# Moving the products of probabilities and values one slot later in an attention and feed-forward kernel

## The reference

```python
c = x @ W.T + b + lora(x, adapter of the sequence)       # cond
q, k, v = c @ wq, c @ wk, c @ wv                         # 32 query heads, 8 k/v heads of 128
q, k = rope(q), rope(k)
p = softmax(mask(q @ k.T * 128**-0.5))                   # causal, within each sequence of 64
x = x + (p @ v) @ wo                                     # attention
m = x @ W2.T + gated lora                                # cond2, top 2 of 8
x = x + m @ base_w.T + base_b + gated lora               # ffn, top 2 of 16
```

## Time and profile before

| what | value |
|---|---|
| median of 3 runs | 2785.87 us (2785.77 to 2792.49) |
| the profiled execution | 2785.09 us, of which 2783.0 us from first to last instruction (the span) |
| TensorE busy with matmuls | 2698.9 us, 97% of the span |
| VectorE, ScalarE, GpSimd busy | 1353.2, 857.3, 1187.6 us |
| mean granted TensorE clock | 0.990 of full speed |

### The profile page before, as it was taken

The page is one execution under the profiler, slowest core; times in us unless marked ns, Lnnn a source line. Parts: engine busy times, 40 slices in busy tenths (PEclk is TensorE's granted clock), DMA queues, the critical chain, the costliest instruction groups (busy, mean ns, idle before and its releaser), DMA issues.

```text
span 2783.0 us, 37584 instructions
## 1 busy us (share of the span) xinstructions
PE 2698.9 (97%) x14520; PEld 2179.5 (78%) x14520; DVE 1353.2 (49%) x2019; ACT 857.3 (31%) x2089; POOL 1187.6 (43%) x782
## 2 busy tenths in 40 slices
PE   8989999999999999999999999999999999999999
PEld 7877777777777788887877777777777778888877
DVE  3134677667777111124533577777777711112552
ACT  2132344444444211221212334444444421121110
POOL 0035765555655245510304475565555434451020
PEclk9999999999999999999999999999999999999999
DMA  6953122122215333111544312222212443311322
GB/s 220 225 184 113 54 76 77 57 69 72 69 62 188 129 114 109 51 39 55 142 123 122 98 54 74 71 77 76 73 57 69 174 136 106 114 46 38 90 87 68
DMA packets 312498, 268.48 MB, mean 96 GB/s; under 512 B 68730, under 2 KB 283898, under 8 KB 312322
## 3 DMA queue, kind: packets, MB, share of 16 engines
q1 hardware_dynamic: 250722, 210.50, 25.1%
q10 hardware_dynamic: 61600, 55.58, 6.0%
HBM read 201.88 MB, written 64.16 MB: 96 GB/s over the span
## 4 chain that ended last, share of the span: by engine, by line
PE 86%; POOL 6%; ACT 3%; DMA 2%; issue 1%; SPq 1%; DVE 1%; ACTq 0%; POOLq 0%; DVEq 0%
PE prod L673 26%; PE prod L675 25%; PE prod L674 25%; PE turned L919 3%; PE turned L869 2%; POOL s_lo L1496 2%; ACT probs L1254 1%; POOL o_lo L1531 1%; PE turned L667 1%; ACT s_hi L1222 1%; PE turned L902 1%; PE prod L1105 1%; POOL w_lo L1461 1%; POOL w_sum L1521 1%; DMA raw<-in_wo 1%
## 5 line engine op out<-in xcount | busy, mean ns | idle before, releaser
L1461 POOL TENSOR_TENSOR w_lo<-raw,w_hi 128x1024 fp32r<-128x1024 f32 x96 | 239.1, 2492 | 815.2 <-ACT w_hi L1165 815.2
L673 PE MATMUL prod<-o_hi,w_hi 128*128 128x512 f32 x1024 | 402.5, 393 | 12.2 <-POOL o_lo L1531 8.6
L675 PE MATMUL prod<-o_hi,w_lo 128*128 128x512 f32 x1024 | 398.7, 389 | 0.0
L674 PE MATMUL prod<-o_lo,w_hi 128*128 128x512 f32 x1024 | 398.6, 389 | 0.0
L1496 POOL TENSOR_TENSOR s_lo<-w_sum,s_hi 128x512 fp32r<-128x512 f32 x192 | 254.4, 1325 | 259.8 <-ACT s_hi L1222 259.8
L1820 DVE TENSOR_TENSOR x<-prod,x 128x512 f32<-128x512 f32 x128 | 88.5, 692 | 562.3 <-PE prod L675 562.3
L673 PE MATMUL prod<-t_hi,s_hi 128*128 128x512 f32 x768 | 314.2, 409 | 12.2 <-POOL s_lo L1496 12.2
L1165 ACT CAST w_hi<-raw 128x1024 fp32r<-128x1024 f32 x130 | 136.0, 1049 | 609.8 <-PE prod L675 431.5
L675 PE MATMUL prod<-t_hi,s_lo 128*128 128x512 f32 x768 | 301.8, 393 | 0.0
L674 PE MATMUL prod<-t_lo,s_hi 128*128 128x512 f32 x768 | 301.3, 392 | 0.0
L673 PE MATMUL prod<-b_hi,s_hi 128*128 128x512 f32 x576 | 241.4, 419 | 0.0
(11 more groups left out here) (168 smaller groups left out, 5067.2 us busy)
## 6 DMA issues: line engine op xcount, KB each, us to landing
raw_pair<-in_wq SPq DMA_DIRECT2D x64, 512.0 KB, 3.6
o_scratch<-o_out ACTq DMA_DIRECT2D x64, 512.0 KB, 2.9
raw<-in_wo SPq DMA_DIRECT2D x64, 512.0 KB, 3.9
o_raw<-o_scratch SPq DMA_DIRECT2D x64, 512.0 KB, 7.1
raw<-t_scratch SPq DMA_DIRECT2D x50, 512.0 KB, 3.6
t_scratch<-x ACTq DMA_DIRECT2D x17, 512.0 KB, 5.6
x_raw<-in_x SPq DMA_DIRECT2D x16, 512.0 KB, 5.8
xt_scratch<-x_sum SPq DMA_DIRECT2D x16, 512.0 KB, 3.3
```

The costliest lines, as they stand in the source:

```text
L673: pe.matmul(dst, wh, xh, start=start, stop=False)
L674: pe.matmul(dst, wh, xl, start=False, stop=False)
L675: return pe.matmul(dst, wl, xh, start=False, stop=stop)
L1461: pool.tensor_tensor(WL[i % 2][:], RAW[i % 2][:], WH[i % 2][:].bitcast(F32), ALU.subtract).then_inc(w_lo, 1)
```

## The change

Five of the items in the two lists, TensorE's and ScalarE's, stand one slot later. No instruction is added, removed or altered.

```diff
                                 if at_ == (QD_KV, 5):
                                     turn_p(gg - 1, 1, 0)
-                                if at_ == (QD_KV, 6):
+                                if at_ == (QD_01, 0):
                                     pv(gg - 1, 0, 0)
-                                if at_ == (QD_01, 0):
+                                if at_ == (QD_01, 1):
                                     turn_p(gg - 1, 1, 1)
-                                if at_ == (QD_01, 1):
+                                if at_ == (QD_01, 2):
                                     pv(gg - 1, 0, 1)
-                                if at_ == (QD_01, 3):
+                                if at_ == (QD_01, 4):
                                     pv(gg - 1, 1, 0)
-                                if at_ == (QD_01, 5):
+                                if at_ == (QD_01, 6):
                                     pv(gg - 1, 1, 1)
                             if at_ == (QD_01, 6):
                                 turn_v(gg, 0)
```

## The result

| | before | changed |
|---|---|---|
| median | 2787.41 us (2785.77 to 2792.49, 5 runs) | 2737.87 us (2736.35 to 2738.77, 5 runs) |
| profiled execution, its span | 2785.09, 2783.0 | 2738.77, 2736.9 |
| TensorE busy | 2698.9 (97%) | 2684.0 (98%) |
| mean granted clock | 0.990 | 0.996 |

The ratio is 0.9816, with a 95% interval of 0.9802 to 0.9829: the change makes the kernel 1.8% faster, and the forecast of 2739 was 1.1 us too high.

What follows compares the result with a forecast made beforehand. TensorE, 97% busy, was taken as the bound, its longest wait at pv 1. Gains of 31.5, 17.0 and 1.7 (50.2 us) less 3.6 for the store gave 46.6, so 2739 us; range 2733 to 2754.

Steps and rivals of the forecast that it cites:

- The wait at pv 1: TensorE's wait for the copy of the turned probabilities goes: 2.25 us per group, 31.5 us over 14 groups.
- The clock: Slow clock in eleven of the 14 stretches around pv 1 goes: 17.0 us, 1.55 us each.
- One item fewer ahead of a product: pv 4 and the first transpose of v stand side by side: 0.12 us per group, 1.7 us over 14.
- The 0.49 us to spare at pv 1: In its new place pv 1 is wanted at 458.13; its input let it go at 457.64, so no wait.
- The store behind pv 3: Issued later, its landing holds up ScalarE, then the second transpose of v: costs 3.6 us, bounds 0 and 18.
- the 3.5: Landing time in us of pv 3's store beyond which the second transpose of v is late.
- GpSimd and the other moved pieces: Product 5's later cast, pv 3's output copy and GpSimd's weights cost nothing; GpSimd's 4.04 us idle covers the weights.
- The rule against it: Frequent small TensorE idles, now before the second transpose of v, can swing the clock; matches a rival of 2772, chance 0.07.

Runs made afterwards that it cites:

- the 1.67 us run: Kernel before, with ScalarE's copy of the turned probabilities that pv 1 needs put ahead of slot (QD_KV, 5)'s cast: 2767.31 us, ratio 0.9918.
- the old slots without a wait: Kernel before, no TensorE item moved; on ScalarE the copy that pv 1 needs goes ahead of slot (QD_KV, 4)'s exponentials: 2738.75 us, ratio 0.9822.
- the later store: Changed kernel with pv 3's output copy on ScalarE at (QD_01, 5) in place of (QD_01, 4), its store issued 0.6 us later: 2742.49 us, single run.

## Why the prediction was right, point by point

- **The wait at pv 1, 31.5 us.** Right, and shown from both sides: it comes back with pv 1 alone put back (30.2 us in 14), and goes with pv 1 alone moved.
- **The clock, 17.0 us.** Right as a term. At pv 1 it hangs on the length of the wait: with 2.17 us the clock fell in 11 and in 12 of 14 groups, with 1.67 in one. At pv 4, with 1.89, it fell in 11. The length doesn't decide alone: in the 1.67 us run the one fall came after 1.66 us, while a wait of 1.76 in another group brought none, and at one place of the `wo` stage waits of 2.11, 2.28 and 2.55 us (before, pv 1 alone, the changed kernel once more) brought none where one of 2.03 did. The prediction took the clock as a price per group that goes with the wait, which holds here because the wait goes entirely.
- **One item fewer ahead of a product, 1.7 us.** Not seen whole. Floor to floor, the changed order and that with pv 1 alone both come to 998.6, and the old slots without a wait to 999.7: it is worth 1.1 us. The first transpose of v takes 0.41 us behind pv 4, from start to start, where it took 0.36 behind a product, and that is the difference, 0.7 over 14.
- **The 0.49 us to spare at pv 1.** Right: in group 2 the copy ended at 454.30, and pv 1 started at 454.94 with no wait before it; less the 0.15 us that lay between the copy's end and pv 1's start before (457.49 and 457.64), that is 0.49. It was enough in all 14.
- **The store behind pv 3, 3.6 us.** The mechanism was right to 0.1 us (issue at 7.98, ScalarE waiting in all 14 groups), and the size was too large. Most stores took 3.3 us where I took 3.8, under the 3.5 from which they were to cost something; in ten of the 14 groups the fourth store of the kernel before had taken 2.9 to 3.3 as well. They cost 1.7 us in the first profile, nearly all in one group, and 0.1 in the second. The 3.5 itself holds: 3.7 us cost 0.2, 5.1 cost 1.6, and with the store issued 0.6 us later 3.2 us cost 0.28 in most groups.
- **GpSimd and the other moved pieces, nothing.** Right: `s_lo` holds TensorE up 10.4 us in 4, all at the starts of the halves as before.
- **The rule against it.** The Trainium skill ("TensorE: Matmul & The Clock Gate", section "A second HAM failure mode: psum-queue depth-cycling") would have had the clock swing with small idles. That is not what the runs show: with a small wait in 12 of the 14 groups, about 0.3 us in ten of them (the later store), and with one of 1.43 in a single group (the changed kernel), the clock stayed at 1.00 in all 14, so the rows decide for the sum. It fell once at 1.66 us, and in most groups at 1.89 and at 2.17.
- The sum, 46.6, stands against 47.6 in the groups and 46.1 in the span. The two small misses (the store 2 us too dear, the item and the clock fall in `wo` 2 us the other way) nearly cancel. Between the medians the gain is 49.5, 2.6 more than was forecast, and the time still came out at 1.1 us, because the kernel before measured higher over 5 runs than over 3. So the last two or three microseconds of the agreement are luck.

## What to carry to other kernels

When an engine that is 97% busy waits for a small copy, look on the copy's engine for what stands ahead of it: one item moved was worth the whole change, and moving the copy on ScalarE did as much. Count a wait of TensorE with what the clock does behind it, since shortening it from 2.17 to 1.67 us paid more than the half microsecond. With a single output buffer, write down for each store when it is issued, what its landing holds up, and from which landing time on somebody feels it; an order that looks looser can bring it within 0.2 us of that.

## What the runs showed of the hardware that I had not expected

- How sharply the fall of the clock at pv 1 depends on the idle time: 1 of 14 groups at 1.67 us, 11 and 12 of 14 at 2.17. What decides between the groups of one run at the same wait is not settled by these runs.
- A slow clock can hide a later wait of the same size (74.85 us for a group with the wait, 74.91 for one with the fall), though not a longer one (76.42 with both).
- A 512 KB store took 2.9 us at the least and in the median of the kernel before, mostly 3.3 when a pair load had been issued 1.7 and 1.3 us before it, and up to 5.1 in the same position.
